# First block's per-batch weights: sixteen register-addressed copies from the table in place of gather, write-back and four copies

## The reference

```
h     = square(relu(hidden @ up_w))            # 256 -> 1024
y     = h @ down_w + (hidden @ expert_w) * (sum of the top 2 of hidden @ gate_w)
out   = x + layernorm(y) * gamma + beta
```

## Time and profile before

| | |
|---|---|
| median of three runs | 239.31 us |
| the profiled execution | 238.72 us |
| its span, first to last instruction | 236.7 us |
| TensorE busy | 226.0 us, 95% |
| VectorE busy | 147.1 us, 62% |
| POOL busy | 132.0 us, 56% |
| ACT busy | 107.2 us, 45% |
| mean granted TensorE clock | 0.989 of full |

### The profile page before, as it was taken

One profiled execution on the slowest core, in us unless ns is written; L12 is line 12 of the kernel. 1 busy time (PEld: TensorE's weight loads), 2 busy tenths in 40 slices (PEclk: granted clock), 3 DMA queues, 4 the chain that ended last, 5 costly groups with the idle time before them and its releaser, 6 DMA issues.

```text
span 236.7 us, 3575 instructions
## 1 busy us (share of the span) xinstructions
PE 226.0 (95%) x1250; PEld 192.8 (81%) x1250; DVE 147.1 (62%) x376; ACT 107.2 (45%) x184; POOL 132.0 (56%) x120
## 2 busy tenths in 40 slices
PE   7689999999999999999999999999999999999990
PEld 2278878888888888888888888888888888888890
DVE  1254787656667666556667666566666666666874
ACT  2248885454444444554455444544445344444100
POOL 4405696456653774465644675365745675467422
PEclk9979999999999999999999999999999999999998
DMA  5679892000200002000110002000020002000211
GB/s 188 199 228 224 173 354 76 4 1 0 83 8 0 1 0 91 1 0 0 51 40 0 3 0 89 1 3 0 15 75 3 0 0 90 3 0 0 79 56 44
DMA packets 15713, 12.95 MB, mean 55 GB/s; under 512 B 5168, under 2 KB 14896, under 8 KB 15696
## 3 DMA queue, kind: packets, MB, share of 16 engines
q1 hardware_dynamic: 15520, 12.14, 16.9%
q0 software_dynamic: 176, 0.59, 0.8%
HBM read 7.94 MB, written 4.78 MB: 54 GB/s over the span
## 4 chain that ended last, share of the span: by engine, by line
PE 85%; DMA 4%; DVE 4%; issue 3%; ACT 1%; POOL 1%; SPq 1%; POOLq 0%; DVEq 0%
PE up_ps L230 36%; PE down_ps L268 22%; PE down_ps L270 12%; PE hid_ps L217 5%; PE moe_ps L286 3%; PE moe_ps L285 3%; PE moe_ps L284 3%; DMA moe<-in_L_cond_weights_dram,cond_col 1%; DMA w_first_by_batch<-moe 1%; POOL rstd L478 1%; DMA cond_col<-in_itok_B_dram 1%; DMA wd<-w_first_by_batch 1%; PE moe_ps L217 1%; DVE hid_lo L361 1%; DVE stats L396 1%
## 5 line engine op out<-in xcount | busy, mean ns | idle before, releaser
L463 POOL TENSOR_TENSOR sq_lo<-square,sq_hi 128x512 fp32r<-128x512 f32 x64 | 83.2, 1300 | 70.6 <-DVE square L369 70.3
L268 PE MATMUL down_ps<-down_hl,sq_hi 128*128 128x512 f32 x248 | 88.7, 392 | 0.0
L270 PE MATMUL down_ps<-down_hl,sq_lo 128*128 128x256 f32 x248 | 69.6, 280 | 0.0
L369 DVE SCALAR_TENSOR_TENSOR square<-up_ps,relu 128x512 f32<-128x512 f32 x64 | 44.0, 687 | 38.2 <-ACT relu L323 38.2
L268 PEld LDWEIGHTS down_ps<-down_hl,sq_hi 128*128 128x128 f32 x248 | 46.5, 188 | 10.6
L323 ACT ACTIVATE relu<-up_ps 128x512 f32<-128x512 f32 x64 | 38.2, 597 | 34.7 <-PE up_ps L230 34.4
L230 PE MATMUL up_ps<-hid_hi,up_hi 128*128 128x512 f32 x128 | 52.2, 408 | 0.0
L230 PE MATMUL up_ps<-hid_hi,up_lo 128*128 128x512 f32 x128 | 50.3, 393 | 0.0
L270 PEld LDWEIGHTS down_ps<-down_hl,sq_lo 128*128 128x128 f32 x248 | 46.7, 188 | 2.4
L325 ACT ACTIVATE sq_hi<-relu 128x512 fp32r<-128x512 f32 x64 | 40.6, 634 | 2.0
L230 PE MATMUL up_ps<-hid_lo,up_hi 128*128 128x512 f32 x128 | 40.3, 395 | 0.5 <-DVE hid_lo L361 0.5
(11 more groups left out here) (44 smaller groups left out, 208.3 us busy)
## 6 DMA issues: line engine op xcount, KB each, us to landing
x_sb<-in_x_dram SPq DMA_DIRECT2D x8, 512.0 KB, 6.6
out_dram<-result SPq DMA_DIRECT2D x7, 512.0 KB, 2.9
result<-in_L_ffn_up_w_dram SPq DMA_DIRECT2D x2, 512.0 KB, 4.6
result<-in_L_ffn_down_w_dram SPq DMA_DIRECT2D x1, 1024.0 KB, 5.6
w_by_batch<-moe SPq DMA_DIRECT2D x1, 512.0 KB, 3.9
out_dram<-result SPq DMA_DIRECT2D x4, 128.0 KB, 1.7
wd<-w_by_batch SPq DMA_DIRECT2D x4, 96.0 KB, 5.9
eg_raw<-L_ffn_expert_weight_dram SPq DMA_DIRECT2D x1, 256.0 KB, 2.7
```

Source lines behind the costliest of these rows:

```text
L268: pe.matmul(dst[:, :], a_hi, down_hl[:, c, :, :].rearrange("p s t -> p (s t)"), start=(c == 0), stop=False)
L270: mm = pe.matmul(dst[:, T:2 * T], a_lo, down_hl[:, c, 0, :], start=False, stop=(c == CH - 1))
L369: dve.scalar_tensor_tensor(square[:, c % 2, :], up_ps[c % UPB][:, :], 0.0, relu[:, c % 2, :], ALU.max, ALU.mult).then_inc(square_done, 1)
L463: pool.tensor_tensor(sq_lo[:, j % 2, c, :], square[:, c % 2, :], sq_hi[:, j % 2, c, :].bitcast(f32), ALU.subtract).then_inc(sq_lo_done, 1)
```

## The change

The sixteen matrices of block 0 are no longer gathered and written back. SP and ACT each load eight indices from DRAM into registers of their own, with a check of their range, and each then issues eight DMAs of one 32 by 32 matrix (4 KB), whose source address in the table is computed from the register and whose target is the matrix's place on the diagonal. SP serves groups 0 and 1, ACT groups 2 and 3, and each group has its own semaphore. The load of up_w's first half moves from SP to ACT, ahead of its index load; up_w's second half is issued on SP behind the eight copies. TensorE conditions block 0 tile by tile, both halves of a tile together, in the order 0, 2, 1, 3, each as its group has landed; the counter of finished halves rises at the last tile. On POOL the memset of the later diagonals comes first, then POOL itself issues the load of the index column, and the gather of all 128 rows waits for the four groups of block 0.

```diff
+FIRST = TILES * Q // 2
...
-        wd_landed = [sem("wd_landed_block0"), sem("wd_landed_block1"), sem("wd_landed_rest")]
+        wd_first_landed = [sem(f"wd_landed_group{g}") for g in range(TILES)]
+        wd_landed = [None, sem("wd_landed_block1"), sem("wd_landed_rest")]
...
+        def conditions(engine, half):
+            mine = cond.rearrange("(o b) -> o b", o=1)[:, FIRST * half:FIRST * half + FIRST]
+            _, rows = nc.values_load_multi_w_load_instructions(mine, [engine], min_val=0, max_val=cond_w.shape[0] - 1)
+            return rows
+
+        def weights_of(row):
+            return cond_w[bass.ds(row, 1), :, :].rearrange("s c d -> (s c) d")
...
-            sp.dma_start(cond_col[:, :], cond.rearrange("(b o) -> b o", o=1)).then_inc(cond_landed, 16)
             sp.dma_start(x_sb[:, groups(0), :], x_rows[:, groups(0), :]).then_inc(x_landed[0], 16)
-            sp.dma_start(up_raw[:, :, up_cols(0)], up_rows[:, :, up_cols(0)]).then_inc(up_landed[0], 16)
-
-            sp.wait_ge(first_gathered, 16)
-            sp.dma_start(first_dram, w_first).then_inc(first_written, 16)
+            rows = conditions(mybir.EngineType.SP, 0)
+            sp.wait_ge(wd_zeroed[0], 1)
+            for n in range(FIRST):
+                g, q = n // Q, n % Q
+                sp.dma_start(wd[C * q:C * q + C, g, D * q:D * q + D], weights_of(rows[n])) \
+                    .then_inc(wd_first_landed[g], 16)
             sp.dma_start(up_raw[:, :, up_cols(1)], up_rows[:, :, up_cols(1)]).then_inc(up_landed[1], 16)
-            sp.wait_ge(wd_zeroed[0], 1)
-            sp.wait_ge(first_written, 16)
-            for q in range(Q):
-                sp.dma_start(wd[C * q:C * q + C, groups(0), D * q:D * q + D], first_by_q[q]) \
-                    .then_inc(wd_landed[0], 16)
...
+            def conditioning_first():
+                pe.wait_ge(x_landed[0], 16)
+
+                for t in (0, 2, 1, 3):
+                    pe.wait_ge(wd_first_landed[t], 16 * Q)
+                    for k in range(K):
+                        mm = pe.matmul(round_bank(0, k)[:, P * t:P * t + P], x_sb[:, t, P * k:P * k + P], wd[:, t, :],
+                                       start=True, stop=True)
+                        if t == TILES - 1:
+                            mm.then_inc(hid_done, 1)
...
-            conditioning(0, 0)
-            conditioning(0, 1)
+            conditioning_first()
...
+            act.dma_start(up_raw[:, :, up_cols(0)], up_rows[:, :, up_cols(0)]).then_inc(up_landed[0], 16)
+            rows = conditions(mybir.EngineType.Activation, 1)
+            act.wait_ge(wd_zeroed[0], 1)
+            for n in range(FIRST):
+                g, q = TILES // 2 + n // Q, n % Q
+                act.dma_start(wd[C * q:C * q + C, g, D * q:D * q + D], weights_of(rows[n])) \
+                    .then_inc(wd_first_landed[g], 16)
             split_up(0)
             split_up(1)
...
+            pool.memset(wd[:, TILES:GROUPS, :], 0.0).then_inc(wd_zeroed[1], 1)
+            pool.dma_start(cond_col[:, :], cond.rearrange("(b o) -> b o", o=1)).then_inc(cond_landed, 16)
             pool.wait_ge(cond_landed, 16)
-            pool.indirect_dma_start(
-                out=w_first, out_offset=None, in_=table,
-                in_offset=bass.IndirectOffsetOnAxis(ap=cond_col[0:TILES * Q, 0:1], axis=0)) \
-                .then_inc(first_gathered, 16)
+
+            pool.wait_ge(wd_first_landed[TILES // 2 - 1], 16 * Q)
+            pool.wait_ge(wd_first_landed[TILES - 1], 16 * Q)
             pool.indirect_dma_start(
                 out=w_all, out_offset=None, in_=table,
                 in_offset=bass.IndirectOffsetOnAxis(ap=cond_col[:, 0:1], axis=0)).then_inc(all_gathered, 16)
-            pool.memset(wd[:, TILES:GROUPS, :], 0.0).then_inc(wd_zeroed[1], 1)
```

More of the change, by code:

```diff
@@ L86, in adaln_ffn @@
         moe_flat = moe[:, :, :, :].rearrange("p a b t -> p (a b t)")
-        w_first = moe_flat[0:TILES * Q, 0:C * D]
         w_all = moe_flat[:, C * D:2 * C * D]
-        first_dram = nc.dram_tensor("w_first_by_batch", [TILES * Q, C * D], f32, kind="Internal").ap()
         all_dram = nc.dram_tensor("w_by_batch", [ROWS_B, C * D], f32, kind="Internal").ap()
-        first_by_q = first_dram.rearrange("(g q) (c d) -> q c g d", q=Q, c=C)
         all_by_q = all_dram.rearrange("(g q) (c d) -> q c g d", q=Q, c=C)
@@ L104, in adaln_ffn @@
             sem, ("cond_landed", "down_landed", "eg_landed", "ln_landed"))
-        first_gathered, all_gathered, first_written, all_written = map(
-            sem, ("first_gathered", "all_gathered", "first_written", "all_written"))
-        wd_landed = [sem("wd_landed_block0"), sem("wd_landed_block1"), sem("wd_landed_rest")]
+        all_gathered, all_written = map(sem, ("all_gathered", "all_written"))
+        wd_first_landed = [sem(f"wd_landed_group{g}") for g in range(TILES)]
+        wd_landed = [None, sem("wd_landed_block1"), sem("wd_landed_rest")]
         result_moved = [sem("result_moved_even"), sem("result_moved_odd")]
@@ L211, in conditioning @@
                     pe.wait_ge(wd_landed[min(j, 2)], 16 * Q)
-                if j > 0:
-                    pe.wait_ge(hid_lo_done, K * j + k)
+                pe.wait_ge(hid_lo_done, K * j + k)
                 for t in range(TILES):
```

## The result

The changed kernel took 244.38 us (median of four, 243.45 to 246.59) against 239.55 of the kernel before (238.66 to 240.37): a ratio of 1.0222, 95% interval 1.0168 to 1.0277. Its profiled execution took 245.24, with a span of 243.1 instead of 236.7.

A forecast was written before the change was run, and what follows sets the result against it. It took the start before steady TensorE work as the bound; gain is the smaller of 1.9 (TensorE's path) and 1.21 + 0.45 - 0.95 = 0.7 (gamma's chain), from 239.31 to 238.6-238.7 us; range 236.6 to 241.7.

The forecast's parts named there:

- POOL's five operations: POOL's gapless chain from block 0's first add of beta to its last sq_lo: 6.95 us, ending at 36.4.
- the cover: Slack between POOL's last sq_lo of block 0 and TensorE's second down product that waits for it: 1.2 us.
- TensorE's own path: Start through the first up round: gains about 1.9 us, second hid_lo ending at 15.4 against 17.29.
- Rival 2: Slow register path makes the kernel slower: 241.7 us at 1.0 us per copy, 253 with separate round trips; chance 0.15.
- the prediction's own signs of being wrong: SP's w_by_batch write issued before 12.3 or after 15, or TensorE waiting elsewhere by more than 1 us.
- The index load and its checks: On SP and ACT before the copies: one 2.0 us round trip for the load, checks inside 0.55 per copy.
- T: Time when all first-block weights have landed: 9.0 us, forecast range 8 to 10.7.
- The copies: Eight 4 KB copies per queue on SP and ACT: 0.55 us each to issue, landing 1.9 us later.
- rival 1: Queue slips little, TensorE's path bounds: gain 1.9 to 3.0 us, 236.3 to 237.4; chance 0.20.
- From T to the gather: POOL's gather of 128 rows starts at 9.05 us, just after the last first-block landing at 9.0.
- The clock: Rival: a TensorE wait brings half clock again, costing 1.7 us, for 240.4; chance 0.05.
- The slip of the queue: SP's transfers behind the w_by_batch write, gamma included, come 0.95 us later: 1.25 less 0.3 given back.

The follow-up runs named there:

- c: The kernel before, with SP issuing beta and gamma after x of blocks 2 to 7, so gamma lands late: 247.85 us, ratio 1.0378.
- d: The changed kernel with its sixteen copies from fixed table rows, no index load or range checks on SP and ACT: 242.61 us, ratio 1.0145.
- n: The changed kernel with up_w's second half issued on SP before its index load: 247.17 us, ratio 1.0364.
- b: The changed kernel without POOL's two waits ahead of the gather of all rows: 241.85 us, ratio 1.0114.
- e: The changed kernel without the eight range checks on SP and on ACT: 241.49 us, ratio 1.0101.
- i: The changed kernel with beta and gamma issued by ACT behind block 0's two hid_hi instead of by SP: 242.25 us, ratio 1.0129.
- j: The changed kernel with copies from fixed rows, gather not gated, beta and gamma on ACT behind block 0's hid_hi: 237.08 us, ratio 0.9912.
- o: As m, but the indices are first loaded as a row of SBUF and the registers filled from there: 236.50 us, ratio 0.9905.
- m: The changed kernel without range checks, up_w's second half before the index load, beta and gamma on ACT behind hid_hi, gather not gated: 240.08 us, ratio 1.0057.

## Why the prediction was wrong

It forecast 238.7, a gain of 0.7, and the kernel lost 4.8. The mechanism that it put in the middle (gate, queue, gamma, POOL's five operations, TensorE's second down group, with 1.2 us of cover) is what happened, and c bears out the cover, though by two differences that cancel. The step that failed is the price of the index load with its checks. It stands in front of both paths, so it made most of the 5.2 us by which gamma's add came later than forecast (34.62 for 29.45), and it turned the gain of TensorE's own path into a loss. Rival 2 named the outcome with a chance of 0.15. Two of the prediction's own signs of being wrong came true: SP's write was issued after 15, at 17.21, and TensorE waited 3.0 us in another place. Term by term:

**The index load and its checks (wrong, the largest).** Priced at 2.0 us as one round trip, with the checks inside the 0.55 per copy. It was 3.5 for the load and 2.1 for the checks, 5.6 in all. The column's DMA row was taken as nearest because it reads the same bytes. It bounds a transfer, not a load into registers, whose pointer is a fetch of its own, and one round trip was the assumption to doubt. The bounds named beside it, nothing to 16 us, held, but the range of the forecast took in only a T of 8 to 10.7.

**The copies (right).** 0.55 per issue against 0.49 (3.88 us for eight), 1.9 from issue to landing against 1.5 to 1.6 (medians).

**T, the last landing (wrong).** 9.0 forecast, 12.1 measured. SP's last copy goes out at 10.60 instead of 7.0 (the load 1.7 more, the checks and the step behind them 2.2 more, the copies' issue 0.3 less) and lands 0.5 sooner after its issue. But d shows that even with no load and no checks T would be 9.7, not 7: x and up_w's first half were named as an argument against rival 1, and then no term of the sum carried them.

**From T to the gather (a term put at nearly nothing).** The prediction starts the gather 0.05 after T. It started 0.8 after, at 12.88 instead of 9.05, and in d and n it is 0.8 again. In the earlier trace rows it is 0.3, from the column's landing at 2.75 to the gather at 3.03. What POOL does in that time is open.

**TensorE's own path (wrong sign).** A gain of 1.9 forecast; 1.5 behind at the first up round, 2.7 by block 1. up_w's second half took 3.9 us, against 3.7 forecast, but it was issued 3.4 later than forecast, behind the same load and checks, and the second hid_lo ended at 19.0, not 15.4. The clock was a rival at 0.05 and came true twice: at 18 to 21 us, after 3.0 us of idle (as after 3.0 in the kernel before), and at 42 to 45, after 2.8. Its price of 1.7 was near the 1.5 lost there.

**The slip of the queue (0.95 forecast, 6.1 measured).** The gather took 4.3 (4.2 forecast). SP's write went out at 17.21 for 13.3, by T and by POOL's 0.8 after it. The write itself took 2.9 instead of 3.9, so it gave back 1.0, the far end of what was allowed for it, and not 0.3. But from the write's issue to gamma's landing the queue took 17.3 us against 16.3, because beta's issue rose from 0.53 to 2.22. Why it did is open; no run isolates it (it is 0.54 in b, 1.15 in n, 1.42 in c, 1.85 in d and 1.86 in e).

**POOL's five operations.** 6.95 forecast, 7.3 measured.

**Sum with the measured start of the gather.** The prediction's own relation is gain = 9.7 - T. The gather's start less the 0.05 of the prediction stands for a T of 12.8, and the gain is -3.1: 242.4, already outside the range. The queue's 1.3 (lost 1.0 where 0.3 was given back) and POOL's 0.35 make it 244.1, of 244.4 measured. That sum ends at the second down group, which the trace has 4.9 later than before. The profiled execution lost 1.5 more behind it and lies 0.9 above the median. Whether the others had the half clock there too isn't known (their mean clocks are 0.975 to 0.989, against 0.972), so that the sum meets the median to 0.3 is in part luck.

**What the forecast would have missed even so.** It took the smaller of two gains. In i, with gamma's chain out of the way, the kernel is still 3.0 slower than before. So with the right index load both of its paths were losses, 4.8 by gamma's chain and 3.0 by TensorE's own.

Of the sentences from the Trainium skill, the one of "Runtime: NRT & Kernel Launch" ("The launch sequence"), some 1.3 us for a load of sequencer registers from HBM, agrees with the 1.31 and 1.21 of the index load alone in the changed kernel (0.9 to 2.8 in the others) and is silent on the 2.20 in front of it. By it the forecast would, as an estimate, have been 0.7 lower, further from what was measured. The one of "DMA: Bandwidth & Descriptors" ("Rules for kernel authors"), that transfers under 64 KB should be coalesced, gave the right sign for a reason that these runs don't bear out: j and o have the same sixteen copies and are faster than the kernel before.

## What to carry to other kernels

When work is gated on something earlier in a queue, follow the last item of that queue (here gamma, 128 KB that nobody looks at) to its first reader, and subtract its cover before counting any gain at the front. A price with no row in the trace that stands in front of two paths at once has to be measured or carried in the range at its full width. And where indices feed DMA addresses, try putting them in SBUF first: with the same 1.5 MB in flight, the load from there took 0.72 us on SP where the load from DRAM took 4.8 (o and m).

## What the runs showed of the hardware

- A load of registers from DRAM shows as two loads, of a pointer and of the values. With x and half of up_w in flight the pointer took 1.5 to 2.2 us, and the two together 3.4 to 3.5 in every run, on SP and on ACT. With another half megabyte they took 4.5 to 4.9 together (pointer 3.5 to 3.9 on SP, 1.7 to 3.6 on ACT). From SBUF there is no pointer fetch, and the eight took 0.72 and 0.73.
- A range check cost a queue 0.26 us: 0.15 of register operations, 0.02 of the assertion, and the steps between them.
- A DMA whose address is in a register took about as long to issue (0.49) as one with a fixed address (0.45, 3.61 us for eight in d).
- A 4 KB copy landed 1.5 us after issue when little else was moving (the changed kernel), 3.1 beside the gather of half a megabyte (b), and 4.2 to 4.4 behind 1 to 1.5 MB (d, o).
- ACT issued DMAs ahead of activations that stand before them in its program. In i the issue of beta stands behind both hid_hi and runs before either:

```profile
15.62 0.37 ACTq L359 DMA_DIRECT2D beta_b<-in_L_ffn_ln_beta_dram  x1
...
16.32 0.58 ACT L318 ACTIVATE hid_hi<-hid_ps 128x512 fp32r<-128x512 f32 x1
16.80 0.59 ACT L318 ACTIVATE hid_hi<-moe_ps 128x512 fp32r<-128x512 f32 x1
```
